# The last layer's token choice, token lists and experts put into one stage

## What is computed

```
scores = softmax(flat_x @ gate_w.T, axis=-1).T          # 16 experts x 4096 tokens
topk_weight, topk_idx = top_k(scores, C)                # C = 4096 * 2 / 16 = 512 tokens for each expert
xg = flat_x[topk_idx]                                   # 16 x 512 x 128
h  = gelu(xg @ Wg.T) * (xg @ Wu.T)                      # 16 x 512 x 512
eo = (h @ Wd.T) * topk_weight[..., None]                # 16 x 512 x 128
out = zeros.at[topk_idx].add(eo)                        # rows added back
shared = (gelu(x @ Sg.T) * (x @ Su.T)) @ Sd.T           # for all tokens
x = x + tanh(g) * (out + shared)
```

## Time and profile before

| what | us |
| --- | --- |
| median of three runs | 1738.68 |
| the profiled execution | 1734.72 |
| its span (first to last instruction) | 1733.0 |
| lists, from the end of the search to the stage's end | 1447 to 1499 |
| experts, first instruction to the last DMA issue | 1500.1 to 1725.7 |

### The profile page before, as it was taken

One profiled execution on the slowest core, in us unless ns is written; L12 is line 12 of the kernel. 1 busy time (PEld: TensorE's weight loads), 2 busy tenths in 40 slices (PEclk: granted clock), 3 DMA queues, 4 the chain that ended last, 5 costly groups with the idle time before them and its releaser, 6 DMA issues. The chain is left out here.

```text
span 1733.0 us, 26948 instructions
## 1 busy us (share of the span) xinstructions
PE 1234.6 (71%) x9767; PEld 847.5 (49%) x9768; DVE 1051.1 (61%) x2108; ACT 770.7 (44%) x1460; POOL 868.2 (50%) x1056
## 2 busy tenths in 40 slices
PE   5480066899842999754799957579998774698884
PEld 4230034555532999544455535445554643555553
DVE  4679783899756011164899867658886498532221
ACT  2357015677641545344566647356665341022220
POOL 4200403666521555465556559445654354258885
PEclk9695577999965999876899979889999695599997
DMA  2000000000003788311000000100000001244442
GB/s 81 14 0 0 0 0 8 1 2 2 2 4 102 196 231 229 102 41 32 2 1 2 2 15 1 36 2 2 2 2 2 10 37 68 74 98 100 97 106 25
DMA packets 51794, 74.93 MB, mean 43 GB/s; under 512 B 8169, under 2 KB 31602, under 8 KB 51282
## 3 DMA queue, kind: packets, MB, share of 16 engines
q1 hardware_dynamic: 35858, 55.01, 9.8%
q0 software_dynamic: 15808, 18.24, 6.5%
HBM read 57.09 MB, written 16.12 MB: 42 GB/s over the span
## 5 line engine op out<-in xcount | busy, mean ns | idle before, releaser
L1571 PE MATMUL ps<-l3f_g_xgT,l3f_g_wu 128*128 128x512 f32 x256 | 118.6, 609 | 0.7 <-ACT l3f_g_xgT L1603 0.7
L1628 DVE TENSOR_TENSOR l3f_g_h<-l3f_g_ga,ps 128x512 f32<-128x512 f32 x64 | 44.0, 687 | 120.4 <-ACT l3f_g_ga L1610 120.4
L587 POOL TENSOR_TENSOR l3x_prob<-l3x_prob,l3x_rden 128x1232 f32<-128x1232 f32 x32 | 71.9, 2248 | 79.1 <-DVE l3x_rden L720 79.1
L1531 POOL DMA_INDIRECT out<-l3f_g_y,l3f_route_slots x64 | 100.2, 1566 | 17.5 <-issue 17.0
L587 POOL TENSOR_TENSOR l2x_prob<-l2x_prob,l2x_rden 128x1232 f32<-128x1232 f32 x32 | 71.9, 2248 | 71.7 <-DVE l2x_rden L720 71.7
L681 ACT ACTIVATE l3x_pt<-ps 77x512 f32<-77x512 f32 x128 | 72.5, 591 | 71.3 <-PE ps L631 71.3
L933 PE MATMUL ps<-l0f_gate,l0f_wT 128*128 x48 | 24.4, 663 | 109.0 <-DVE l0f_gate L852 108.9
L1996 DVE TENSOR_TENSOR l1f_g_y<-ps,l1f_g_wd 128x256 f32<-128x256 f32 x39 | 16.6, 424 | 140.5 <-PE ps L1952 140.5
L587 POOL TENSOR_TENSOR l1x_prob<-l1x_prob,l1x_rden 128x1232 f32<-128x1232 f32 x32 | 71.9, 2248 | 58.2 <-DVE l1x_rden L720 58.2
L681 ACT ACTIVATE l2x_pt<-ps 77x512 f32<-77x512 f32 x128 | 72.6, 591 | 52.1 <-PE ps L631 52.1
L1979 ACT ACTIVATE l1f_g_h<-ps,l1f_g_wd 128x256 f32<-128x256 f32 x156 | 62.9, 475 | 72.2 <-DMA l1f_g_wd<-l1f_W 46.6
(11 more groups left out here) (485 smaller groups left out, 3544.3 us busy)
## 6 DMA issues: line engine op xcount, KB each, us to landing
l1f_g_wd<-l1f_W SPq DMA_DIRECT2D x39, 322.0 KB, 3.9
l1f_g_wu<-l1f_W SPq DMA_DIRECT2D x39, 256.0 KB, 3.8
l3f_g_wu<-l3f_W SPq DMA_DIRECT2D x16, 512.0 KB, 4.1
l1f_y_rows<-l1f_g_y SPq DMA_DIRECT2D x39, 128.0 KB, 4.0
l3f_g_wd<-l3f_W SPq DMA_DIRECT2D x16, 256.0 KB, 2.9
l3f_rows<-l3f_route_own_rows SPq DMA_DIRECT2D x1, 2304.0 KB, 6.9
sb_x<-x SPq DMA_DIRECT2D x1, 2048.0 KB, 7.5
l1f_rows<-l1f_route_own_rows SPq DMA_DIRECT2D x1, 2048.0 KB, 9.5
```

The source lines that it names most:

```text
L587: pool.tensor_tensor(prob[n % 4][:], prob[n % 4][:], rden[n % 2][:].unsqueeze(2).broadcast_to([P, HEADS, KEYS]), ALU.mult).then_inc(normed, 1)
L1531: pool.indirect_dma_start(out=out_rows, out_offset=spot(g, i), in_=y[g % 2][:, i, :], in_offset=None, compute_op=ALU.add).then_inc(added, 16)
L1571: ins = pe.matmul(bank(c, i), wu[g % W][:, (i * C + c) * P:(i * C + c + 1) * P], xgT[g % 2][:], start=True, stop=True)
L1628: v.tensor_tensor(h[g % 2][:, c, :], ga[c % 2][:], bank(c, 1), ALU.mult).then_inc(h_ready, 1)
```

## The change

`choose_tokens` and `token_experts` become one stage, `token_layer`, with one set of semaphores. The lists of experts 0 to 3 are made ahead of the first expert; the list of expert g+4 is made in the course of expert g. `take` now works on one expert. Several buffers share memory with ones that are no longer in use (`junk`, `seg_score`, `h` in `xc`; `xh` in `xnT`; `y` in `shared`, `xgT` in `up_sb`, `gx` in `ga`). The turned rows have one PSUM bank instead of two, the lists two. The tiny gelu at the stage's start is gone. The bodies of `load_rows`, `add_rows`, `up_x`, `gelu_x`, `multiply_x` and `weigh` are those of before with new names of semaphores, but that `load_rows` also waits for its own list (`taken`).

```diff
+    W, R, AHEAD = 3, 4, 4
+        def list_bank(e):
+            return 5 if e < AHEAD and e % 2 else 7
         @block.sync
             sp.wait_ge(weighed, 1)
             sp.dma_start(u["rows"].rearrange("(p n) f -> p n f", p=P), rows[:]).then_inc(rows_stored, 16)
-            sp.wait_ge(x_stored, 16 * NBLK)
-            sp.wait_ge(rows_stored, 16)
+            for g in range(E):
+                p = g % W
+                if g >= W:
+                    sp.wait_ge(x_made, CX * (g - W + 1))
+                sp.dma_start(wu[p][:], d["l3f_W"][g, :, 0:NUP]).then_inc(wu_came[p], 16)
+                if g >= W:
+                    sp.wait_ge(x_down, g - W + 1)
+                sp.dma_start(wd[p][:], d["l3f_W"][g, :, NUP:WIDTH]).then_inc(wd_came[p], 16)
         @block.gpsimd
...
             for q in range(E // QE):
                 at = slice(q * QE * NT, (q + 1) * QE * NT)
                 pool.wait_ge(hi_hot_ready, q + 1)
                 pool.tensor_tensor(hi_num[:, at, 1, :]...).then_inc(hi_tile_ready, 1)
+            def load_rows(g):
+                pool.wait_ge(taken, g + 1)
...
+            pool.memset(zero[:], 0.0).then_inc(load_step, 1)
+            pool.wait_ge(rows_stored, 16)
+            pool.wait_ge(x_stored, 16 * NBLK)
+            for g in range(R):
+                load_rows(g)
+            for g in range(E):
+                add_rows(g)
+                if g + R < E:
+                    load_rows(g + R)
         @block.tensor
-            for e in range(E):
+            def list_tokens(e):
                 pe.wait_ge(hi_token_ready, e // QE + 1)
                 pe.wait_ge(hi_tile_ready, e // QE + 1)
                 pe.wait_ge(lo_ready, e + 1)
+                if e >= 2:
+                    pe.wait_ge(taken, e if e > AHEAD else e - 1)
                 for i in range(CH):
+                    ins = pe.matmul(ps[:, list_bank(e), 0:2 * NHI], lo_hot[e % 2][:, :, i], hi_num[:, e * CH + i, :, :]...)
                 ins.then_inc(listed, 1)
+            def turn_rows(g):
+                pe.wait_ge(row_came[g % R], 16 * TB * (g // R + 1))
+                if g >= 1:
+                    pe.wait_ge(row_kept, g)
+                for i in range(TB):
+                    ins = pe.transpose(ps[:, 6, i * P:(i + 1) * P], xg[g % R][:, i, 0:D], ident[:])
+                ins.then_inc(row_turned, 1)
...
+            for e in range(AHEAD):
+                list_tokens(e)
+            turn_rows(0)
+            for g in range(E):
+                up_x(g, 0)
+                up_x(g, 1)
+                if g + 1 < E:
+                    turn_rows(g + 1)
+                up_x(g, 2)
+                up_x(g, 3)
+                if g + AHEAD < E:
+                    list_tokens(g + AHEAD)
+                if g >= 1:
+                    down_x(g - 1)
+            down_x(E - 1)
         @block.vector
+            def take(e):
+                v.wait_ge(listed, e + 1)
+                nums = ps[:, list_bank(e), 0:2 * NHI]
+                step(v.tensor_scalar(slot[e % 2][:], nums[:, 0:NHI], float(NT), -float(NT), ALU.mult, ALU.add))
+                step(v.tensor_tensor(slot[e % 2][:], slot[e % 2][:], nums[:, NHI:2 * NHI], ALU.add))
+                v.tensor_scalar(u["slots"][:, e * G:(e + 1) * G], slot[e % 2][:], 0.0, None, ALU.max).then_inc(taken, 1)
...
             low_hot(0)
             v.wait_ge(chosen, 1)
             step(v.scalar_tensor_tensor(hi[:], hi[:], 1.0, sel[:], ALU.add, ALU.mult))
             high_hot(0)
             low_hot(1)
+            take(0)
+            low_hot(2)
+            take(1)
+            low_hot(3)
+            take(2)
             high_hot(1)
-            low_hot(2)
+            low_hot(4)
+            take(3)
             high_hot(2)
-            low_hot(3)
             high_hot(3)
-            for e in range(4, E):
-                low_hot(e)
-                if e % QE == 2:
-                    take(e // QE - 1)
-            take(E // QE - 1)
+            for g in range(E):
+                if g >= 2:
+                    weigh(g - 2)
+                for c in range(CX):
+                    multiply_x(g, c)
+                if g + AHEAD < E:
+                    take(g + AHEAD)
+                if g + AHEAD + 1 < E:
+                    low_hot(g + AHEAD + 1)
+            weigh(E - 2)
+            weigh(E - 1)
```

More of the change, by code:

```diff
@@ L1153, in _, with token_layer @@
             sc.activation(p2[:], p2[:], ACT.Exp).then_inc(exp_ready, 1)
-def choose_tokens(nc, u, d, E, K, gate_at, out):
+def token_layer(nc, u, d, E, K, gate_at, out):
     STEPS, HIGH = 15, 8
@@ L1182, in choose_tokens @@
             s.one("out_kept"), s.one("added"), s.one("x_stored"), s.one("rows_stored"))
+        wu_came, wd_came = ([s.one(f"{n}{p}") for p in range(W)] for n in ("wu_came", "wd_came"))
+        row_came = [s.one(f"row_came{p}") for p in range(R)]
+        taken, row_turned, row_kept, x_made, x_acted, x_ready, x_down, y_ready, y_added, load_step, add_step = (
+            s.one(n) for n in ("taken", "row_turned", "row_kept", "x_made", "x_acted", "x_ready", "x_down", "y_ready", "y_added", "load_step", "add_step"))
         def sb(name, shape, dt=F32):
@@ L1191, in choose_tokens @@
         top, total = sb("top", [P, NT]), sb("total", [P, NT])
[L1192 removed]
+        seg_score, seg_count = u["xc"][:, 3 * E * NT:4 * E * NT], sbs("seg_count", [P, 3], 2)
+        junk = [u["xc"][:, k * E * NT:(k + 1) * E * NT] for k in range(3)]
         high, low, found, reached, nextf, ordinal = sb("high", [P, 1]), sb("low", [P, 1]), sb("found", [P, 1]), sb("reached", [P, 3]), sb("nextf", [P, 3]), sb("ordinal", [P, 3])
@@ new lines, in down_x @@
+            def down_x(g):
+                pe.wait_ge(x_ready, CX * (g + 1))
+                pe.wait_ge(wd_came[g % W], 16 * (g // W + 1))
+                if g == 1:
+                    pe.wait_ge(taken, AHEAD)
+                if g >= 2:
+                    pe.wait_ge(y_ready, g - 1)
+                for i in range(TB):
+                    for c in range(CX):
+                        ins = pe.matmul(ps[:, 4 + g % 2, i * P:(i + 1) * P], xh[g % 2][:, c, i * P:(i + 1) * P], wd[g % W][:, c * P:(c + 1) * P],
+                                        start=(c == 0), stop=(c == CX - 1))
+                ins.then_inc(x_down, 1)
@@ L1395, in _ @@
             v.wait_ge(seg_turned, 1)
-            step(v.tensor_copy(seg_score[:], ps[:, 3, :]))
+            step(v.tensor_copy(seg_score, ps[:, 3, :]))
             for j in range(STEPS):
@@ L1455, in high_hot, with multiply_x, weigh @@
                                 flat(hi)[:, at].unsqueeze(2).broadcast_to([P, QE * NT, NHI]), ALU.is_equal).then_inc(hi_hot_ready, 1)
[L1457 to L1464, removed]
+            def take(e):
[4 more added lines that the diff above has]
+                v.tensor_scalar(u["slots"][:, e * G:(e + 1) * G], slot[e % 2][:], 0.0, None, ALU.max).then_inc(taken, 1)
+            def multiply_x(g, c):
+                v.wait_ge(x_acted, CX * g + c + 1)
+                if g >= 2 and c == 0:
+                    v.wait_ge(x_down, g - 1)
+                v.tensor_tensor(xh[g % 2][:, c, :], gx[c % 2][:], ps[:, 2 * (c % 2) + 1, :], ALU.mult).then_inc(x_ready, 1)
+            def weigh(g):
+                v.wait_ge(x_down, g + 1)
+                if g >= 2:
+                    v.wait_ge(y_added, 16 * TB * (g - 1))
+                v.scalar_tensor_tensor(y[g % 2], ps[:, 4 + g % 2, :].rearrange("p (i d) -> p i d", d=D), gate,
+                                       xg[g % R][:, :, D + g:D + g + 1].broadcast_to([P, TB, D]), ALU.mult, ALU.mult).then_inc(y_ready, 1)
             low_hot(0)
```

207 lines of the change are left out of this document (60 added, 147 removed).

## The result

After the change the kernel takes 1729.82 us (median of 15 runs, 14 of them from 1725.93 to 1734.87; one took 2554.49 and is left out of the ratio), before 1740.47 (15 runs beside them, 1734.03 to 1749.34). The ratio is 0.9938, 95% interval 0.9923 to 0.9954. It is faster by some 11 us where I forecast 27, and lies above my range. The profiled execution took 1726.67, its span 1725.0. The gain did not keep its size: beside each other on a later chip the two kernels took 1759.66 and 1762.25, ratio 0.998 (0.9962 to 0.9997).

A forecast was written before the change was run, and what follows sets the result against it. GpSimd's round of 12.77 us was taken to bound the experts. Span 1733.0 - 26.6 + 0 + 0 + 1.0 = 1707.4, 1709.1 with 1.7 around it; 1712 was taken between 1709.1 and 1713.1, range 1704 to 1725.

The forecast's parts named there:

- The first gather: Ahead of the experts: GpSimd's first gather comes 26.6 us earlier, at 1474.2, bounds 25 to 28.
- The start: First experts: a turn 2.2 us better against two lists of 1.1 us each; sum 0, bounds -0.2 and +1.9.
- The port: Experts' stage: VectorE's moved operations hold none of GpSimd's gathers, load-steps or add-steps; no cost.
- rival C: Experts: `low_hot` holds GpSimd's gathers, eleven times up to 2.29 us, +25, so 1725 to 1738; chance 0.09.
- the late expert: Experts: one whose turn waits 3.20 us costs more with less slack; +1.0 for one or two, bounds 0 and +4.
- The list on TensorE: Between up and down products: a list costs 1.1 us at full clock, hidden in the steady part; upper bound 2.0.
- rival B: Experts: the loop or TensorE becomes the bound, rounds of 13.7 us, +10.7, so 1717 to 1723; chance 0.15.
- D: Experts: a list lets TensorE's granted clock fall in every expert, twelve times, +138, near 1850; chance 0.04.
- the end: Last four experts: they have no list and go as before.

The follow-up runs named there:

- the pieces of 16 and 32 rows: Kernel after, each `low_hot` of experts 5 and up cut into eight instructions of 16 rows (1720.1 us, ratio 0.9867) or four of 32 (1748.15 us, 0.9939).
- b1: Kernel before plus an unused bf16 compare with two SBUF inputs on VectorE behind the last multiply of experts 0 to 10: 1757.81 us, ratio 1.0079.
- b2: Kernel before plus an unused bf16 reduce with one input on VectorE behind the last multiply of experts 0 to 10: 1739.16 us beside 1742.43.
- b5: Kernel before plus an unused f32 copy with one input on VectorE behind the last multiply of experts 0 to 10: 1777.98 us beside 1760.68.
- b6: Kernel before plus an unused f32 addition with two inputs on VectorE behind the last multiply of experts 0 to 10: 1778.93 us beside 1760.68.
- the 8 pieces: Kernel after, each `low_hot` of experts 5 and up as eight instructions of 16 rows: ratio 0.9867, on later chips 0.9925 and 0.9931.
- The list by itself: Kernel before plus 32 unused bf16 products ahead of the down products of experts 0 to 11, nothing added on VectorE: 1770.45 us, ratio 1.0029.
- beside the adds: Kernel after, with `low_hot` behind the second multiply of an expert instead of the fourth: 1737.53 us, ratio 0.997.

## Why the prediction was wrong

*The first gather: right.* 27.3 us earlier against 26.6 forecast. Counted from `low_hot(0)`, GpSimd's second product starts at 15.45 (forecast 15.7), the fourth ends at 21.7 (22.4). Two products were held for a whole `low_hot` and took 3.05, as in the earlier trace rows.

*The start: right on the first chip,* +0.8 in bounds of -0.2 to +1.9. Where the same stage was profiled again it was +5.2, but between two chips. In the kernel after TensorE, ScalarE and VectorE stand still together in the first expert; ScalarE and TensorE, from the second profile:

```profile
1518.71 0.22 PE L1461 MATMUL ps<-topk_hi_num,topk_lo_hot 128*128 128x8 bf16 x1 [0.71 <-issue]
...
1518.74 0.60 ACT L1387 ACTIVATE topk_ga<-ps 128x512 f32<-128x512 f32 x1 [3.60 <-remote]
...
1521.54 6.51 PE L1481 MATMUL ps<-topk_up_sb,topk_wu 128*128 128x512 f32 x8 [1.95 <-issue]
```

These waits name nothing that the profile shows. The kernel before, again, has a shorter one there (ScalarE 2.62 us), and no run tells what they are.

*The port, my name for whatever lets VectorE hold GpSimd up: this step failed.* I wrote "So nothing is held", against rival C, on two grounds. The earlier trace rows have VectorE pieces of 0.28 us; if a gather is held to the end of the piece it meets, such pieces can't show it, and that is the rule the pieces of 16 and 32 rows then showed (0.25 and 0.5 us held). And I placed `low_hot` between a load-step and an add-step, looked only whether those two were hit, and passed over the four gathers that stand between them. The earlier trace rows were the nearest rows, a GpSimd instruction that reads SBUF beside a whole `low_hot`; I gave the case they speak for 0.09. C's mechanism was right and its price twice too high: it said up to 2.29 us a time, +25 in eleven. Measured is 0.98 to 1.92, 13.2 in nine, because the gather starts 0.3 to 1.2 us after `low_hot`. With that, my 1709.1 without its 1.0 for the late expert, plus 13.2, is 1721.3, and with the 5.7 us of the earlier stages 1727, the profiled execution. So it is partly luck that C's 1725 to 1738 holds the measured time.

The runs b1, b2, b5 and b6 show what holds a gather: an instruction with two SBUF inputs (up to 2.96 us in b1, 3.14 in b6) and an f32 copy (2.96 in b5), and not the reduce (1.02 at most in b2). Whether it is the gather's reading of its list in SBUF that is held or another part of its work, no run tells, nor what in the two engines makes the one wait for the other.

*The list on TensorE: mis-sized.* 1.1 taken, 1.9 measured. I scaled with the clock, from the earlier trace rows, the 99 ns of another stage; the list's loads stay at 163, so a list's time does not go with the clock. That puts 13.0 on TensorE against 12.77, and the loop at 23.8 + 1.9 = 25.7 against 25.54, which is rival B. B put a round at 13.7; the 8 pieces run at 13.72 in the mean on the last chip, 13.31 on the first. In the kernel as changed B is mostly hidden behind C: taking C away gave back 8.4 us of 12.6 by the first profiles and 7.0 of 16.3 by the last, and what is left, 4 and 9, is B with the pieces' own short holds in it (seven gathers of 1.17 to 1.22 in the last). The list by itself cost 6 to 7.

*The late expert:* priced at +1.0, bounds to +4. The kernel before has one such round in ten, 14.03, and none when profiled again. With a list such rounds become frequent (14.45 to 14.7). But the late expert's up products took 5.30 us, at a granted clock of 0.72 from 1614 to 1620, and those of the alternating rounds 3.60, so whether it is the same thing as B is not shown.

*The clock* stayed at 1.00 (D fell), and the end went as before, 61.8 us.

## What to carry to other kernels

Before you lay work beside an engine without slack, look for what makes the one slow the other besides the semaphores: here a gather of 0.95 us took up to 2.87 beside a `low_hot`. Read its price from a row in which a piece of the same length stands beside the same kind of instruction. If VectorE must run beside GpSimd's gathers, cut it into pieces of some 0.3 us: here VectorE paid 0.5 us more a list, and the kernel took 1750.25 us beside 1759.66. And put work of TensorE where TensorE waits anyway, ahead of the wait, not on the way from what it waited for to what others wait for: here that took the alternation out of the rounds, though no gain in the whole's time could be told.

## What the runs showed of the hardware

- A gather (0.95 us), an add (1.55) and a one-column operation (0.2 to 0.8) of GpSimd were held to the end of a long VectorE instruction (2.28 to 2.39 us) with two SBUF inputs or of an f32 copy, up to 3.14 us (b6), 3.56 (beside the adds) and 2.80 (b1). A gather that began 0.04 us or more inside it ended 0.81 to 0.90 us after it, an add 1.41 to 1.45 (beside the adds); four that began within its first 0.03 us took 0.95 to 0.98.
- A reduce with one SBUF input (2.41 us, b2) and a multiply with one input from SBUF and one from PSUM (0.69 us, the kernel before) held no gather (0.95 to 1.02).
- A weight load of 128 x 128 in bf16 with a product of 8 columns took 61 ns at a granted clock of 0.50 (3.92 us for 64, the kernel before) and 58 at 1.00 (1.87 us for 32, the kernel after).
- TensorE's granted clock was 0.75 from 1552 to 1558, a stretch with a wait of 2.21 us for rows, when its down products had been halved; with all of them and a wait of 1.97 it was 1.00 from 1568 to 1574. In the kernel before it was 0.72 from 1614 to 1620, behind a wait of 3.20.
